# Batch 0's attention preparation written out per engine, heads 0 to 7 ahead of heads 8 to 15

## What is computed

```python
x = x + 0.5 * ffn(layernorm(x), ...)      # 8 experts, capacity 512 rows, switch routing
x = x + attn(layernorm(x), ...)
x = x + 0.5 * ffn(layernorm(x), ...)

def attn(x, wq, wk, wv, wproj, g_rms):     # 16 heads of 16, B = 8, T = 1024
    q, k, v = x @ wq.T, x @ wk.T, x @ wv.T
    q, k = rms(q), rms(k)                  # over the 16 values of a head, times g_rms
    q, k = rope(q), rope(k)                # [u1*cos + u2*sin, -u1*sin + u2*cos]
    scores = einsum('bhtd,bhsd->bhts', q, k) / 4 + 1.0
    y = einsum('bhts,bhsd->bhtd', softmax(scores), v)
    return y @ wproj.T
```

## Time and profile before

| | |
|---|---|
| time of the kernel before | 2294.75 us, median of 3 (2292.65 to 2299.19) |
| the profiled execution's own time | 2278.68 us |
| its span, first to last instruction | 2276.8 us |
| PE busy | 2101.2 us (92%) |
| DVE busy | 1745.3 us (77%) |
| ACT busy | 1702.5 us (75%) |
| POOL busy | 944.1 us (41%) |

### The profile page before, as it was taken

The page is one execution under the profiler, slowest core; times in us unless marked ns, Lnnn a source line. Parts: engine busy times, 40 slices in busy tenths (PEclk is TensorE's granted clock), DMA queues, the critical chain, the costliest instruction groups (busy, mean ns, idle before and its releaser), DMA issues.

```text
span 2276.8 us, 35911 instructions
## 1 busy us (share of the span) xinstructions
PE 2101.2 (92%) x12776; PEld 1062.3 (47%) x12776; DVE 1745.3 (77%) x2662; ACT 1702.5 (75%) x3309; POOL 944.1 (41%) x1073
## 2 busy tenths in 40 slices
PE   4579965899999999999999999999999999997997
PEld 2369854343444344434434443443434333335896
DVE  7657645788887988888798788879888898726674
ACT  6856643478888888788888878888887887865663
POOL 4755413263383265158227614832661101204441
PEclk7589986899999999999999999999999999999998
DMA  8733511425434433453333434343333444112431
GB/s 271 262 131 131 191 51 54 94 30 132 71 67 106 88 67 104 81 94 76 95 87 67 96 82 87 74 104 65 79 94 58 84 71 96 50 29 92 142 127 50
DMA packets 144994, 218.02 MB, mean 96 GB/s; under 512 B 32128, under 2 KB 101178, under 8 KB 144560
## 3 DMA queue, kind: packets, MB, share of 16 engines
q1 hardware_dynamic: 135216, 197.99, 35.9%
q0 software_dynamic: 9216, 16.95, 2.1%
q10 hardware_dynamic: 384, 0.79, 0.2%
HBM read 129.66 MB, written 84.79 MB: 94 GB/s over the span
## 4 chain that ended last, share of the span: by engine, by line
PE 79%; DVE 10%; ACT 3%; issue 3%; DMA 3%; POOL 2%; SPq 0%; ACTq 0%; POOLq 0%; DVEq 0%
PE PS L968 20%; PE PS L952 19%; PE PS L935 12%; PE PS L879 7%; DVE NMX L1948 5%; PE PS L721 3%; PE PS L910 3%; PE PS L848 3%; PE PS L850 3%; PE PS L849 3%; PE PS L832 2%; PE PS L834 2%; PE PS L833 2%; PE PS L975 1%; DMA NX<-in_x 1%
## 5 line engine op out<-in xcount | busy, mean ns | idle before, releaser
L1948 DVE TENSOR_REDUCE NMX<-PS 128x1 f32<-128x1024 f32 x1024 | 1221.8, 1219 | 241.8 <-PE PS L935 236.8
L1368 ACT ACTIVATE PB<-PS 128x512 f32<-128x512 f32 x2048 | 1098.1, 604 | 209.9 <-PE PS L952 199.3
L952 PE MATMUL PS<-QF,KF 51*128 51x512 f32 x2048 | 791.5, 462 | 6.0 <-ACT SQ L1323 2.9
L935 PE MATMUL PS<-KF,QF 49*128 49x512 f32 x2048 | 705.0, 442 | 21.7 <-DVE NMX L1948 16.0
L952 PEld LDWEIGHTS PS<-QF,KF 51*128 51x128 f32 x2048 | 324.9, 184 | 553.3 <-ACT PB L1368 315.3
L968 PE MATMUL PS<-PB,V 128*17 128x512 f32 x4096 | 540.5, 599 | 0.2
L935 PEld LDWEIGHTS PS<-KF,QF 49*128 49x128 f32 x2048 | 312.2, 186 | 150.0 <-DVE NMX L1948 93.5
L2173 POOL TENSOR_TENSOR R1R<-R,HI 128x512 fp32r<-128x512 f32 x60 | 76.8, 1281 | 199.0 <-ACT R L1334 198.9
L1712 DVE TENSOR_TENSOR HLR<-HL,HHR 128x512 fp32r<-128x512 f32 x128 | 88.8, 694 | 87.5 <-ACT HHR L1297 87.5
L848 PE MATMUL PS<-W2H,HLR 128*128 128x256 f32 x512 | 142.8, 279 | 0.0
L850 PE MATMUL PS<-W2H,HHR 128*128 128x256 f32 x512 | 141.5, 276 | 0.0
(11 more groups left out here) (268 smaller groups left out, 3050.4 us busy)
## 6 DMA issues: line engine op xcount, KB each, us to landing
W<-in_w SPq DMA_DIRECT2D x32, 1024.0 KB, 8.0
QF<-qs SPq DMA_DIRECT2D x186, 128.0 KB, 4.2
KF<-qs SPq DMA_DIRECT2D x186, 128.0 KB, 6.9
qs<-HI SPq DMA_DIRECT2D x64, 256.0 KB, 2.1
qs<-R1R SPq DMA_DIRECT2D x64, 256.0 KB, 2.5
buf<-ZT SPq DMA_DIRECT2D x16, 520.0 KB, 10.5
PX<-x2d SPq DMA_DIRECT2D x8, 1024.0 KB, 5.5
QX<-x2d SPq DMA_DIRECT2D x8, 1024.0 KB, 5.7
```

Source lines behind the costliest of these rows:

```text
L935: m = e.matmul(PS[:, 2 * i + half, :], QF[k][at:at + ROWS_S, p * SEQ + ti * 128:p * SEQ + ti * 128 + 128], KF[k][at:at + ROWS_S, p * SEQ + ...
L952: e.matmul(PS[:, bank, :], KF[k][at:at + ROWS_ST, p * SEQ + sbk * 128:p * SEQ + sbk * 128 + 128], QF[k][at:at + ROWS_ST, p * SEQ + th * 51 ...
L1368: e.activation(PB[j % 3][:, h * 512:(h + 1) * 512], PS[:, place["e", tile], :], ACT.Exp).then_inc(e_out, 1)
L1948: e.tensor_reduce(NMX[:, u % 2, at:at + 1], PS[:, 2 * i:2 * i + 2, :], AX.XY, ALU.max, negate=True).then_inc(s_max, 1)
```

## The change

Ahead of the main loop each engine gets a function `lead` in place of the generators of batch 0:

- The load of `PX` is issued as two halves of four row tiles; statistics, power and normalisation go half by half. VectorE normalises (before: ScalarE). The two GpSimd operations that made the bias are left out.
- The low part of the transposed rows is VectorE's, read from PSUM; ScalarE's second copy (`XTP`) is left out.
- `QK0` and `SQ0` hold all eight row tiles, in memory of the exponentials. VectorE sums, rotates and scales only heads 0 to 7 (operations of 2x128 columns). GpSimd takes the roots in two parts of 64 columns for each row half; behind those of heads 0 to 7 it rotates heads 8 to 15, takes their roots and scales them.
- Pieces 0 to 3 have four buffers (`HI0`, `LO0` are new), their low part is read from PSUM, the copy `R1` is left out, and the high part is stored as soon as it is there. Six of the eight value tiles are projected ahead of or between the pieces.
- Eight filler matmuls stand ahead of TensorE's first transposes (`AGAIN[10]`). Seven banks of PSUM rotate there (`RING_LEAD`), three before.
- In the main loop pieces 4 to 7 of batch 0 move from steps 0, 1, 2, 4 to 13, 14, 15, 17; batch 1's preparation begins at step 6 instead of 4, is loaded to a buffer of its own (`PX1`) and is normalised by ScalarE (before: GpSimd).

VectorE, ahead of the main loop, before: one row tile of all 16 heads (rotation, then the sum of the next).

The low parts of pieces 4 to 7 and batch 1's power stand behind all of this on GpSimd now. The core of the diff:

```diff
-PIECES_0 = ((40, 0, 0), (41, 0, 2), (42, 1, 0), (43, 1, 2), (0, 1, 1), (1, 1, 3), (2, 0, 1), (4, 0, 3))
+PIECES_0 = ((0, 0, 0), (0, 0, 2), (0, 1, 0), (0, 1, 2), (13, 1, 1), (14, 1, 3), (15, 0, 1), (17, 0, 3))
-BEGIN = {1: 4, 2: 55, **{b: BATCH * (b - 1) - EARLY for b in range(3, 8)}}
+BEGIN = {1: 6, 2: 55, **{b: BATCH * (b - 1) - EARLY for b in range(3, 8)}}
```

SyncE:

```diff
+            def lead():
+                for h in range(2):
+                    part = slice(4 * h, 4 * h + 4)
+                    e.dma_start(PX[:, part, :], rows(x2_d, 0)[:, part, :]).then_inc(ld_half if h else ld_px, 16)
+                for _ in stores(0, 0, 4):
+                    pass
...
```

TensorE:

```diff
+            def lead():
...
+                e.wait_ge(pn_ve, 1)
+                again(AGAIN[10], V_BANK)
+                for g in range(3):
+                    across(0, g)
+                e.wait_ge(wq_lo, 1)
+                both(0, 0)
+                across(0, 3)
+                for t in range(1, 8):
+                    both(0, t)
+                piece = split(0, 0, 4)
+                next(piece)
+                for k, first, last in ((0, 0, 3), (2, 3, 6)):
+                    for t in range(first, last):
+                        value(0, t)
+                    next(piece)
+                    next(piece, None)
+                for t in range(6, 8):
+                    value(0, t)
+                again(AGAIN[9], V_BANK)
...
```

ScalarE:

```diff
+            def lead():
+                ones(0)
+                for g in range(4):
+                    e.wait_ge(xt_full, g + 1)
+                    e.copy(XTH[:, :, g * 256:(g + 1) * 256],
+                           PS[:, place["xt", g], :].rearrange("p (a n) -> p a n", a=2)).then_inc(xt_raw, 1)
+                for t in range(8):
+                    e.wait_ge(qk_full, t + 1)
+                    e.copy(QK0[:, t, :], PS[:, place["qk", t], :]).then_inc(qk_out, 1)
+                    e.activation(SQ0[:, t, :], PS[:, place["qk", t], :], ACT.Square).then_inc(qk_sq, 1)
...
```

VectorE, behind the statistics:

```diff
+                e.wait_ge(pn_rs, 1)
+                for i in range(4):
+                    normal(i)
+                e.wait_ge(pn_rs, 2)
+                normal(4)
+                lower(0)
+                normal(5)
+                lower(1)
+                normal(6)
+                normal(7)
+                lower(2)
+                lower(3)
...
+                summed(0, 0)
+                for t in range(7):
+                    turn_begun(e, own, t, 0)
+                    summed(t + 1, 0)
+                    own.wait(e)
+                    turn_ended(e, own, t, 0)
+                turn_begun(e, own, 7, 0)
+                own.wait(e)
+                e.wait_ge(rq_root, 1)
+                for t in range(4):
+                    scaled(e, t, 0)
+                turn_ended(e, own, 7, 0)
+                own.wait(e)
+                e.wait_ge(rq_root, 2)
+                for t in range(4, 8):
+                    scaled(e, t, 0)
+                for _ in split(0, 0, 4):
+                    pass
+                for t in range(8):
+                    summed(t, 1)
```

GpSimd:

```diff
+                for h in range(2):
+                    part = slice(4 * h, 4 * h + 4)
+                    e.wait_ge(pn_ve, h + 1)
+                    e.tensor_tensor(RS[:, 0, part], VE[:, 0, part], NEGH[:, 0:4], ALU.pow).then_inc(pn_rs, 1)
...
+                for m in range(2):
+                    root(m, 0)
+                for t in range(8):
+                    turn_begun(e, own, t, 1)
+                    own.wait(e)
+                    turn_ended(e, own, t, 1)
+                for m in range(2):
+                    root(m, 1)
+                own.wait(e)
+                e.wait_ge(rq_root, 4)
+                for t in range(8):
+                    scaled(e, t, 1)
```

More of the change, by code:

```diff
@@ L671, in sync_program @@
             e.wait_ge(yo_done, 4 * NE)
+            lead()
             side = Side()
-            side.begin(0, before(0))
-            for n in range(BATCH):
-                side.run(n)
             for n in range(NS + LAST + 1):
@@ L1995, in vector_program @@
             e.memset(PS[:, V_BANK, :], 0.0).then_inc(set_up, 1)
-            prepare(side, 0, 0, pre_x, split)
-            for n in range(BATCH):
-                side.run(n)
+            lead()
             for n in range(NS + LAST):
```

286 lines of the change are left out of this document (180 added, 106 removed).

## The result

| | before | after |
|---|---|---|
| median of the runs | 2295.39 us (7 runs, 2290.37 to 2299.19) | 2280.62 us (7 runs, 2275.82 to 2284.37) |
| ratio | | 0.9938, 95% interval 0.9924 to 0.9953 |
| profiled execution, its span | 2278.68, 2276.8 | 2283.36, 2281.5 |

The change makes the kernel faster by 14.8 us (0.62%); forecast were 21.7. The time lies in the range of 2264 to 2283, so the sign and the place were right and the size was two thirds of what was said. Two of the signs that the prediction named beforehand did not hold: a root took 10.1 us where it said that one above 8 would make it wrong, and the first score came 0.8 us behind the stretch that it gave (374 to 382 us, which is +46.7 to +54.7 behind the load).

The account below looks back on a forecast made before the run. Bound: a chain of waits from batch 0's load to the first score, 74.0 us, no engine filled. First score 23.0 us earlier, minus 1.3 for the clock, gives 21.7: 2294.75 to 2273 us, range 2264 to 2283.

Parts of the forecast that it names:

- Two of the signs: Would make the prediction wrong: a root above 8 us; expected in the profile after: first score at 374 to 382 us.
- Load in halves: Batch 0's load ahead of the main loop: first statistics at 331.0 instead of 333.3 us; warming matmuls cost nothing.
- Normalisation, first projection: From statistics to TensorE's first projection: VectorE normalises by halves, first projection at 339.6 instead of 345.8 us.
- VectorE's loop: Sums and rotations per row tile: 1.45 us instead of 2.60, last sum at 355.4 instead of 370.1; the largest term.
- Root: GpSimd's root behind the last sum, on 64 columns: 6.3 us, between 5.3 and 8.6, ending at 361.7.
- The second rival: GpSimd's root becomes the bound, operations not shrinking with columns, 8.6 us each; gain 16.1, 2279 us; chance 0.18.
- Scaling of tiles 4 to 7: VectorE's scaling behind the root: 1.3 us alone, 4.3 waiting out GpSimd operations; taken as 3.0, ending at 364.7.
- Pieces and loads: From scaling to first score: pieces out 5.8 us instead of 9.4, loads 7.8; first score at 378.3 instead of 401.3.
- Behind the first score: Main loop: GpSimd's heads 8 to 15 and batch 1's later beginning cost nothing; TensorE's clock costs 1.3 us.
- rivals 4 and 5: 4: later batch 1 and stores eat the gain, 2290 to 2300 (0.03); 5: GpSimd late at step 13, 2298 (0.03).
- Rival 3: TensorE stays at 1.2 GHz in the projections and eight more steps; gain 8 us, 2287 us; chance 0.07.

Follow-up runs that it names:

- held kernel: Changed kernel with GpSimd waiting until heads 0 to 7 are scaled before turning heads 8 to 15; tiles 4 to 7 scaled in 1.43 us, first score at +53.60.
- the repeat: The changed kernel timed and profiled once more, with no edit; ratio to the kernel before 0.9948 (0.9935 to 0.9961).

## Why the prediction was right, and where not

*Load in halves.* Forecast 2.3 us, measured 1.4 (4.63 against 6.04; the one-load kernel gives the same 1.4). The line between a 256 KB store and a 1 MB load promised too much: the first half landed 4.6 us after its issue, not 3.4, with the second half, landed 5.6 us after its own issue, under way beside it. The claim that the eight warming matmuls cost nothing holds only in the balance: they stand on the path for 1.2 us and give it back in the projections.

*Normalisation, first projection.* 1.1 late, of which 0.9 is the load. By the loop's beginning it is recovered.

*VectorE's loop.* The largest term, and right in the main: 1.40 us per pass for 1.45, the last sum ended at +27.0 for +28.1. The 1.1 us that it had charged here for GpSimd's root beside the loop came to nothing. (Its terms add up to 355.8, not 355.4: 344.2, seven passes, one sum and the 1.1.)

*Root.* The step that failed, a term of 6.3 us that measured 10.0: 4.7 us in which the second root waited for the first, which the forecast put at nothing, and 5.3 for the second root itself. The forecast had the first root done by the last sum. It added 1.0 us to a root alone, for contention, on the pattern of the rotations of before, which both engines shared with some loss each. It put one price on "beside VectorE". There are two: beside sums with idle time between them a root takes 5.2 us, beside rotations with small gaps 6.4, beside this gapless loop 10.1. The forecast itself had made the loop gapless when it let the wait for VectorE's own result be covered by the next tile's sum; it did not ask what the gaps had been good for. The second rival had the shape right (the first root ends after the last sum, the second behind it, a gain of 16.1 us) and a wrong reason: it had operations that stay long when the width is halved. They don't: alone they take 0.24 to 0.33 and the second root 5.3, the forecast's number for a root alone. Its time of 2279 is nearer to the measured 2280.62 than the forecast's 2273, and it is this rival, taken into the range, that helped to carry the range to 2283.

*Scaling of tiles 4 to 7.* 3.0 forecast, 2.93 measured, and the held kernel shows that 1.5 of it is contention.

*Pieces and loads.* 5.8 us became 6.8 and 7.8 became 8.7. Both are stretches of issues and landings; repeats of the same work vary by 0.9 to 1.5 us (single store issues of 1.4 to 1.8 us for 0.45 in three profiles).

*Behind the first score.* The forecast charged 1.3 for the clock and nothing else. Over the eight profiles with step 6 and the two of before the stretch up to the first exponential is 61.2 us for 60.8 and the rest 1818.8 for 1816.2: 3.0 in all. 1.4 to 1.8 of it, 1.6 in the mean, is batch 1's later beginning, which the forecast cost at nothing. The other 1.4 stays open, the 0.4 ahead of the first exponential included: two profiles of before are few against jumps of 1.6 us. GpSimd's heads 8 to 15 were scaled 71 us behind the load (step 13's matmuls began some 30 us later), and no wait of TensorE for GpSimd is in the trace: forecast 72, right, and rivals 4 and 5 out. Rival 3 is out in the projections, which ran at 1.00; its other half, more steps at the low clock, was there in some executions (0.50 over 44 us in after), and in the mean it comes to those 0.4 us at most.

The sum: the first score at +73.7 before and +56.0 after (means of two profiles each), 17.7, less 3.0 is 14.7; timed were 14.8 and, in the repeat, 13.0.

## What to carry to other kernels

Before a chain of small GpSimd operations is started early beside VectorE, look at what VectorE does in that time: if it streams two-input operations without a gap, GpSimd gets one operation in whenever a single-input one comes by, and the early start brings the end of the chain forward by little; put waits there (what sums alone would do, without idle time between them, no run here shows), hold GpSimd back from what is next on the path, or give the chain to VectorE. After a term has been taken off a chain, read what stands in the in-order queues of the next engines between the old and the new time: what was hidden there (18 value matmuls, 3.5 us) is the next bound. And a fixed order of work that is moved "by two steps, at no cost" can have its price far behind: 1.4 us here, by step 69.

## What the runs showed of the hardware that was not expected

VectorE is not slowed at all by GpSimd in the gapless loop (pass 1.40 us with and without it), while GpSimd's 0.24 to 0.33 us become 1.1 to 1.4. Where VectorE waits a little between operations both are slowed, by up to 0.13 us an operation. In the scaling, where the operations of both are long, VectorE's 0.34 become 0.7.

VectorE does the 14 dependent operations of the root on 128 columns in 4.2 us, GpSimd in 7.4 (its first operation, beside VectorE, 1.14 of it) and on 64 columns in 5.3.

TensorE's granted clock over the 44 us behind the first score was 0.78 and 0.66 in two executions of the kernel before (idle for 4.9 and 4.5 us ahead of it), 0.50 and 0.66 in two of the changed one (9.8 and 10.6 us): 3.4 us from first score to first exponential between two executions of one program, in either kernel, that no edit explains. The idle time ahead shows, if at all, in the first 10 us (0.70 against 0.50 to 0.59). A single profile with a higher clock over the whole stretch, as that of the kernel with 48 fillers, doesn't price the edit.
